# RWKV attention and a mixture of experts on one core: the attention periods' steps in a new order, with a chunk's preceding sums added by two transfers in place of one

## The reference, cut to what matters

```python
xk = x * time_mix_k + shifted * (1 - time_mix_k)      # xv, xr alike
k, v, r = xk @ Wk.T, xv @ Wv.T, xr @ Wr.T
# per token, with num, den, mx carried along:
mo  = maximum(mx, kt + u)
out = (exp(mx - mo) * num + exp(kt + u - mo) * vt) / (exp(mx - mo) * den + exp(kt + u - mo))
ms  = maximum(mx + w, kt)
num = exp(mx + w - ms) * num + exp(kt - ms) * vt       # den alike, without vt
y = (sigmoid(r) * out) @ Wo.T
```

## Time and profile before

| what | us |
|---|---|
| median of 3 runs | 1244.07 (1239.03 to 1246.96) |
| the profiled execution | 1250.05 |
| its span, first to last instruction | 1248.3 |
| from the start to the last `refined` of the attention | 511.3 |

### The profile page before, as it was taken

One profiled execution on the slowest core, in us unless ns is written; L12 is line 12 of the kernel. 1 busy time (PEld: TensorE's weight loads), 2 busy tenths in 40 slices (PEclk: granted clock), 3 DMA queues, 4 the chain that ended last, 5 costly groups with the idle time before them and its releaser, 6 DMA issues.

```text
span 1248.3 us, 16083 instructions
## 1 busy us (share of the span) xinstructions
PE 1117.1 (89%) x5320; PEld 832.2 (67%) x5320; DVE 838.5 (67%) x1951; ACT 750.2 (60%) x1279; POOL 331.8 (27%) x295
## 2 busy tenths in 40 slices
PE   5969989899989967899999889999998998999893
PEld 3546646473646544488888778888887886878761
DVE  4798988888798877689887944454444444444384
ACT  2666979698888888653332245565565555546353
POOL 2021121212222121200000034433434443344355
PEclk9989999899999977899999999999999999999996
DMA  8412364453635266676363069979888987887798
GB/s 320 175 34 67 56 158 71 138 101 102 140 76 105 68 142 157 151 218 241 139 208 111 5 213 244 256 239 257 247 231 263 245 240 235 220 243 185 186 317 329
DMA packets 87972, 222.52 MB, mean 178 GB/s; under 512 B 10704, under 2 KB 10832, under 8 KB 85072
## 3 DMA queue, kind: packets, MB, share of 16 engines
q1 hardware_dynamic: 59424, 156.98, 35.8%
q0 software_dynamic: 28464, 64.50, 28.0%
HBM read 145.93 MB, written 59.28 MB: 164 GB/s over the span
## 4 chain that ended last, share of the span: by engine, by line
PE 28%; DMA 18%; DVE 6%; issue 3%; ACT 2%; POOL 1%; POOLq 0%; SPq 0%; DVEq 0%; ACTq 0%
DMA ysh<-k_sb,mixf 13%; PE bank L734 5%; PE bank L709 3%; PE bank L711 2%; PE bank L710 2%; PE bank L691 2%; PE bank L692 2%; PE bank L693 2%; DMA xnd<-ysh 2%; DMA xnd<-h,mixf 1%; PE bank L537 1%; PE bank L723 1%; PE bank L749 1%; PE bank L751 1%; PE bank L750 1%
## 5 line engine op out<-in xcount | busy, mean ns | idle before, releaser
L1387 POOL DMA_INDIRECT ysh<-k_sb,mixf x64 | 115.7, 1807 | 202.3 <-DMA ysh<-k_sb,mixf 115.3
L598 PE MATMUL bank<-mix_ring,weights 128*128 128x512 f32 x288 | 133.5, 617 | 19.4 <-DVE mix_ring L1489 19.4
L605 PE MATMUL bank<-weights,rw 128*128 128x512 f32 x256 | 118.8, 620 | 13.8 <-ACT sr L863 11.4
L1133 ACT ACTIVATE k_sb<-bank 128x512 f32<-128x512 f32 x64 | 38.2, 597 | 140.5 <-PE bank L693 140.5
L598 PEld LDWEIGHTS bank<-mix_ring,weights 128*128 128x128 f32 x288 | 56.3, 198 | 91.1 <-issue 67.4
L1363 POOL DMA_INDIRECT xres<-h,mixf x48 | 54.1, 1127 | 221.7 <-DVE mixf L1928 210.4
L1942 DVE TENSOR_TENSOR run_max<-run_max 128x256 f32<-128x256 f32 x64 | 27.3, 426 | 118.9 <-ACT e_split L1169 118.9
L1327 POOL DMA_DIRECT2D wkv<-recur x31 | 38.0, 1225 | 254.5 <-DVE recur L1554 254.5
L691 PE MATMUL bank<-h_high,ffn_w 128*128 128x512 f32 x256 | 102.7, 401 | 2.7 <-ACT k_sb L1133 2.7
L605 PEld LDWEIGHTS bank<-weights,rw 128*128 128x128 f32 x256 | 50.9, 200 | 78.5 <-issue 63.5
L709 PE MATMUL bank<-ffn_w,s_split 128*128 128x512 f32 x256 | 101.9, 398 | 0.1
(11 more groups left out here) (253 smaller groups left out, 2737.4 us busy)
## 6 DMA issues: line engine op xcount, KB each, us to landing
wkv<-in_w SPq DMA_DIRECT2D x96, 512.0 KB, 5.1
state<-in_w SPq DMA_DIRECT2D x32, 512.0 KB, 4.7
wkv<-recur POOLq DMA_DIRECT2D x31, 512.0 KB, 5.3
h<-xres SPq DMA_DIRECT2D x8, 1024.0 KB, 4.2
xin<-h SPq DMA_DIRECT2D x8, 1024.0 KB, 6.3
xin<-in_x SPq DMA_DIRECT2D x7, 1024.0 KB, 9.3
xres<-in_x POOLq DMA_DIRECT2D x7, 1024.0 KB, 11.7
x<-xres SPq DMA_DIRECT2D x7, 1024.0 KB, 4.5
```

Source lines behind the costliest of these rows:

```text
L598: mm = pe.matmul(bank[:, d, :], W(j)[:, ck, d * P:(d + 1) * P], mix_slot(4 * j + ck), start=(ck == 0), stop=(ck == CK - 1))
L605: mm = pe.matmul(bank[:, s, :], rw[:, ck, s * P:(s + 1) * P], W(3)[:, ck, :], start=(ck == 0), stop=(ck == CK - 1))
L1387: pool.indirect_dma_start(t["ysh"], bass.IndirectOffsetOnAxis(ap=scatter_token[:, e % IB:e % IB + 1], axis=0), e_out[q], None, compute_op= ...
```

## The change

In all four blocks the helper functions are cut into single steps (one instruction or one chunk each; each returns at once where its tile does not exist), and `period` is a plain list of them in a new order. PE's list is in the old order; its waits for a PSUM half are replaced by a wait for each bank ahead of the first matmul into it. `add_prev` issues two accumulating transfers of 256 KB. `den_scan` loses its wait for `boosted`, and `y_squares` its wait for `x1_squared` (the latter has a scratch tile of its own, `x1_junk`). The first and the last periods get their extra steps at other places. Some semaphores are merged to make room for two new ones. No arithmetic changes.

PE, the waits for one bank at a time (k, transposed x and y alike):

```diff
-            def output(bank, tau, ck):
+            def output(tau, ck):
                 pe.wait_ge(S["rw_ready"], 4 * tau + ck + 1)
                 for s in range(ST):
+                    if ck == 0:
+                        if has(tau, 1):
+                            pe.wait_ge(S["r_ready"], 4 * (tau + 1) + s + 1)
...
```

POOL:

```diff
             def add_prev(tau, c):
                 u = CK * tau + c
+                pool.wait_ge(S["boosted"], u + 1)
                 pool.wait_ge(S["r_times_v"], u + 1)
+                pool.wait_ge(S["scanned"], 2 * u + 1)
+                pool.dma_start(unit[:, c % 2, R, :], sums_of[:, c % 2, 1, 0:TT], accum_op=ALU.add).then_inc(S[f"den_added{u % 2}"], 16)
                 pool.wait_ge(S["scanned"], 2 * u + 2)
-                pool.dma_start(unit[:, c % 2, NUM:R + 1, :], sums_of[:, c % 2, :, 0:TT], accum_op=ALU.add).then_inc(S[f"prev_added{u % 2}"], 16)
+                pool.dma_start(unit[:, c % 2, NUM, :], sums_of[:, c % 2, 0, 0:TT], accum_op=ALU.add).then_inc(S[f"num_added{u % 2}"], 16)
...
+                if has(tau, 0): add_prev(tau, 0)
+                if has(tau, 2) and not first(tau): scale_and_offset(1, tau + 2)
...
```

ACT, the new list of a middle period (steps of the first and the last periods left out):

```diff
+                v_round(tau + 1, 0)
+                if has(tau, 0): ln3_row(tau - 2, 0)
+                if has(tau, 0): ln3_row(tau - 2, 1)
...
+                if has(tau, 0): ln3_row(tau - 2, 2)
+                above(tau, 1)
+                below(tau, 1)
+                carry_over(tau, 0)
+                exp_both(tau, 1)
+                room(tau, 1)
+                if has(tau, 0): ln3_row(tau - 2, 3)
+                boost(tau, 1)
+                v_round(tau + 1, 1)
+                v_round(tau + 1, 2)
...
+                seed(tau, 2)
+                recip_log(tau, 0)
...
+                ln1_row(tau + 2, 0)
+                ln1_row(tau + 2, 1)
+                ln1_row(tau + 2, 2)
+                k_read(even, tau + 1, 0)
+                k_read(even, tau + 1, 1)
+                ln1_row(tau + 2, 3)
+                k_read(even, tau + 1, 2)
+                k_read(even, tau + 1, 3)
...
+                recip_exp(tau, 0)
+                above(tau, 2)
+                below(tau, 2)
+                carry_over(tau, 1)
+                exp_both(tau, 2)
+                if has(tau, 0): y_square(tau - 1, 0)
...
+                v_round(tau + 1, 3)
+                if has(tau, 0): y_square(tau - 1, 3)
+                room(tau, 2)
+                recip_log(tau, 1)
+                seed(tau, 3)
+                boost(tau, 2)
+                r_round(tau + 1, 0)
...
+                recip_exp(tau, 1)
+                if has(tau, 0): y_scale(tau - 1, 0)
...
+                r_round(tau + 1, 1)
+                v_read(tau + 1, 0)
...
+                above(tau, 3)
+                r_round(tau + 1, 2)
+                below(tau, 3)
+                r_round(tau + 1, 3)
+                xnT_read(tau + 2, 0)
...
+                exp_both(tau, 3)
+                carry_over(tau, 2)
+                room(tau, 3)
+                boost(tau, 3)
+                seed(tau + 1, 0)
...
+                recip_log(tau, 2)
+                recip_exp(tau, 2)
...
+                if has(tau, 0): x1_square(tau - 1, 0)
+                if has(tau, 0): x1_square(tau - 1, 1)
+                if has(tau, 0): x1_square(tau - 1, 2)
...
+                above(tau + 1, 0)
+                below(tau + 1, 0)
+                exp_both(tau + 1, 0)
+                r_reads(tau + 1)
+                if has(tau, 0): x1_square(tau - 1, 3)
+                room(tau + 1, 0)
+                boost(tau + 1, 0)
+                carry_over(tau, 3)
+                recip_log(tau, 3)
+                recip_exp(tau, 3)
...
+                seed(tau + 1, 1)
```

DVE, the same (`e_times_v` is line 1533 of before, `recip_times_sum` and `recip_times_num` are 1578 and 1580):

```diff
+                if not first(tau): ln1_row_stats(tau + 2, 0)
+                mix(tau + 1, VJ, 0)
+                if not first(tau): ln1_row_stats(tau + 2, 1)
+                den_scan(tau, 0)
+                e_times_v(tau, 0)
+                r_times_v(tau, 0)
+                num_scan(tau, 0)
...
+                gap_scan(tau, 1)
...
+                gap_taken(tau, 1)
...
+                if not first(tau): recip_times_num(tau - 1, 3)
...
+                if not first(tau): ln1_moments(tau + 2)
+                if not first(tau): recip_times_sum(tau - 1, 3)
...
+                if not first(tau): refined(tau - 1, 3)
+                mix(tau + 1, VJ, 1)
+                mix(tau + 1, VJ, 2)
+                den_scan(tau, 1)
...
+                v_rest(tau + 1, 2)
...
+                num_gated(tau, 0)
...
+                recip_times_sum(tau, 0)
+                recip_times_num(tau, 0)
+                mix(tau + 1, VJ, 3)
+                refined(tau, 0)
+                mix(tau + 1, RJ, 0)
+                den_scan(tau, 2)
...
+                v_rest(tau + 1, 3)
+                mix(tau + 1, RJ, 1)
+                e_times_v(tau, 2)
+                num_scan(tau, 2)
+                r_rest(tau + 1, 0)
+                r_times_v(tau, 2)
+                mix(tau + 1, RJ, 2)
+                gap_scan(tau, 3)
+                mix(tau + 1, RJ, 3)
+                gap_taken(tau, 3)
+                shift(tau + 2)
+                r_rest(tau + 1, 1)
+                num_gated(tau, 1)
+                recip_times_sum(tau, 1)
+                recip_times_num(tau, 1)
+                r_rest(tau + 1, 2)
+                refined(tau, 1)
+                diff(tau + 2, 0)
+                diff(tau + 2, 1)
+                r_rest(tau + 1, 3)
+                mix(tau + 2, KJ, 0)
+                den_scan(tau, 3)
+                e_times_v(tau, 3)
+                r_times_v(tau, 3)
+                num_scan(tau, 3)
+                gap_scan(tau + 1, 0)
+                gap_taken(tau + 1, 0)
...
+                mix(tau + 2, KJ, 1)
+                num_gated(tau, 2)
...
+                num_gated(tau, 3)
...
+                mix(tau + 2, KJ, 3)
```

703 lines of the change are left out of this document (352 added, 351 removed).

## The result

The kernel after takes 1195.6 us (median of 4 runs, 1192.1 to 1200.0) where the kernel before, run beside it, takes 1245.5: ratio 0.9595, 95% interval 0.9523 to 0.9666.

A forecast was written before the change was run, and what follows sets the result against it. PE was taken to bound the kernel, with 52.8 us the least per middle period. Gains of 18.4 + 0.5 + 4.0 + 7.6 = 30.5 took 1250.05 to 1219.5, minus 6.0 to 1213.5, stated as 1215 us; range 1203 to 1237.

The forecast's parts named there:

- The chain through the residual and the seed: Middle periods: with the seed ahead of `x1_square`, PE's `mix_ring` wait goes; periods fall from 58.6 to 54.0, 18.4 us.
- PE's least: Middle periods: PE is busy 52.8 us at full clock, so no period can be shorter than 52.8.
- Fifth period: The period with no tile left to normalise, 53.3 us long, gains 0.5 us.
- Period 0: Statistics of tile 2 move ahead of four mixes; PE's v starts at 77.2, not 82.80; 4.0 us counted, between 1 and 7.
- The finer waits of PE: PE waits per PSUM bank: up to 1.6 us where ACT is late, in middle periods inside the 54.0.
- The split: Two transfers per unit for one: early denominator worth nothing, price nothing up to a landing of about 7 us.
- The last two periods: Attention's end: 1 for PE's reads of r, 4.2 for `boosted`, 2.4 for two moved steps; 7.6 us, bounds 0 and 12.
- The wait for `boosted`: Last tile: `den_scan` waits for `exped` instead, 1.4 us earlier for three units, 4.2 us.
- (a): Rival, middle periods: the loops of PE, DVE and ACT disturb each other; periods of 56.5, time 1230 us; chance 0.20.
- (b): Rival: residual lands later, ACT stands at `x1_square`, PE's wait moves and keeps its length; 1238 us; chance 0.12.
- (c): Rival: a fixed time per transfer makes the second half 2.8 us later, `seed(tau, 2)` 1.5 late; 1222 us; chance 0.10.
- (d): Rival, slower: two halves land at 16 us or later, ACT stands at `seed(tau+1, 0)`; 1260 us; chance 0.08.

The follow-up runs named there:

- e2: Kernel after with ACT's seed of the next tile's unit 0 put back behind three of the four x1 squares; 1208.7 us, ratio 0.9707.
- e3: Kernel before with ACT's seed of the next tile's unit 0 put ahead of the four x1 squares; 1229.6 us, ratio 0.9872.
- e17: Kernel after with the residual's 1 MB transfer issued as two of 512 KB, the first two x1 squares waiting for the first alone; 1195.4 us, ratio 0.9597.
- e5: Kernel after, but PE waits for all four banks of a PSUM half ahead of the first matmul into it; 1199.1 us, ratio 0.9634.
- e8: Kernel after with one transfer of 512 KB per unit in tiles 0 to 5 and two of 256 KB in tiles 6 and 7; 1199.1 us, ratio 0.9629.
- e14: Kernel after with one accumulating transfer of 512 KB per unit in place of two, same code as e1; 1203.5 us, ratio 0.9665.
- e6: Kernel after with `den_scan` waiting for `boosted` again; 1238.6 us, ratio 0.9939.
- e9: Kernel before, order kept, but the denominator scan no longer waits for `boosted`; e*v waits for `room`, r*v for `boosted`; 1245.7 us, ratio 1.0019.
- e15: Kernel after with each of a unit's two transfers cut in two, four of 128 KB; 1205.9 us, ratio 0.9690.
- e1: Kernel after with one accumulating transfer of 512 KB per unit in place of two; 1201.8 us, ratio 0.9665.

## Why the prediction came out too small, point by point

**The chain through the residual and the seed: right.** The wait for `mix_ring` went, the granted clock is 1.00 in every middle period, and the seed is there before `gap_scan`, as the walk had it. e2 and e3 show it from both sides. It isn't the whole of the middle's gain: alone it earns 2.7 of the 6.0 us a period (e3).

**PE's least: the step that failed.** The forecast said that "a middle period can't be shorter than 52.8" and set 54.0 on it. e17's periods of 50.3 refute it. The row of 57.60 us in the earlier trace rows has two marks that I passed over. It counts 180 PE records, where the others have 176 to 178 and a period's own are 176 (32 each of k and of output, 48 each of v and of r, 16 transposes): the cut caught four matmuls of v more. And PE stood three times in it, and each restart adds to "busy" time: the groups of k took 3.59 and 7.13 us around a wait, where the same 24 records in one run take 10.46 (PE's timelines of before and after). Four records at 0.23 us and, as an estimate, three restarts at those 0.26 make 1.7 of the 2.5; the rest I did not trace. With PE's 52.8 out of the way, DVE's loop was the bound; the walk had 52.1 for it and it is 52.4. With 52.1 as the base the same sum gives 52.1 + 1.2 = 53.3, so that of the 1.4 us a period 0.7 go to PE's least and 0.7 to the 1.2 for "delays of one pass to another". Together they are 4 x (54.0 - 52.6), 5.5 us of the miss.

**Fifth period: "PE's full work does fit into 53" was the same error.** Its 50.75 of PE in 53.3 left room for 2.5, and I gave it 0.5. It gained 4.1 and is now 49.2 long, below those 50.75. 3.6 us of the miss.

**Period 0: right mechanism, mis-sized.** v starts at 76.20 (said 77.2), 6.6 us earlier. The 2.4 us held back for `ffn_rest` were wrong: at the period's end nothing waits for it, and PE runs from 81.2 to 132.8 without a stop. The gain was 7.2, at the upper bound of 7. 3.2 us of the miss.

**The finer waits of PE: right for the middle, short for the ends.** In the middle nothing (e5). At the ends about 1.5 and 5 us in one profile of e5, of which the forecast had counted a part in period 0; the times don't show them.

**The split: half right.** "The early denominator is worth nothing in this order" holds for middle periods of 52.3 us, and there "the price of the split is also nothing" holds too (e8, e14). The +0.8 us for the second half was too careful: a half lands in 4.0, so the second lands about as early as the whole did. In the tail the split is worth 5.2 us, most of it through the numerator of unit (6, 3) and about 2 through the denominator of unit (7, 1). What failed in this part is a term of the last two periods, where I named the landing of unit (6, 3)'s sums and counted "nothing beyond 1". Rival (e), the split doing nothing, falls.

**The last two periods.** 10.0 in place of 7.6, and the terms can't be checked one by one against it. Put back into the new order, the whole transfer costs 5.2 us of this stretch (e14), the wait for `boosted` over 7 (e6) and the coarse waits of PE 5.0 (e5), over 17 together: they overlap. In the old order taking `boosted` away gave 1.3 (82.5 in e9), against the 4.2 of the forecast. That the sum came within 2.4 us of the measured gain is therefore luck in part. PE's wait for r fell from 11.42 to 5.73, the routing's from 9.33 to 8.61.

**The wait for `boosted`.** The forecast used it in the last tile only. Shown is that nearly the whole gain of the new order hangs on its going (e6, 38 to 43 us), and that in the old order it is worth nothing (e9). Pricing a change edit by edit, each against the old order, can't find this.

**The rivals.** (a), loops in each other's way, did not happen: 52.6. (b) was the right place with a small price: the residual does land later (13.3), ACT does stand there, and the period pays 2 us for it (e17), not the whole gain. (c) and (d): no wait of a seed for its sums shows in the kernel after or in e15 with its four transfers. The Trainium skill (DMA: Bandwidth & Descriptors, section on the anatomy of one DMA on the SWDGE path) would make a half 0.6 us shorter than a whole, an estimate from its 436 GB/s; the rows have 5.3, 4.0 and 3.5 us for 512, 256 and 128 KB, 1.3 and 0.5 us less. The same page of the Trainium skill, in its rules for kernel authors, advises to coalesce many small transfers into one large one; here two of 256 KB in place of one of 512 KB earn 5 us of the tail in the profile.

**The scale.** The 6.0 us by which the profile of before lay over the median match the part behind the attention, which was at the long end there (737.0 of 724 to 737), so subtracting them fits the record. The misses are 5.5 + 3.6 + 3.2 + 2.4 = 14.7; with the 1.5 added for small waits they make 16.2 of the 19.4 us from 1215 to 1195.6. The other 3 are within the scatter of the medians (1195.6 and 1200.7 for the same kernel). The low end of the range counted a gain of 41 us; the attention gained 45.0, and what lies beyond is the fifth period's 3.6.

## What to carry to other kernels

PE's busy time in a window is no floor while PE still stops in it: compare the record counts and add up an unbroken run of each kind of matmul. Price a removed wait in the new order, not in the old: the same wait was worth 0 us in one and about 40 in the other. Where engines are within 5% of each other, look for the last wait on a transfer in the loop and try letting its first users wait for the first half only (e17: 2.1 us a period in the profile, not shown in the time). Here a split transfer shortened the stretch where a unit's chain stands alone, and in e15 it cost through its issues on the queue, by what stood behind them.

## What the runs showed of the hardware beyond that

The residual's transfer of 1 MB landed in 10.9 to 13.3 us (medians) over the kernels above, and in 11.9 and 12.9 in two executions of one kernel (e1, e14), whose middle periods were 51.5 and 52.3. Over the kernels with ACT's middle list unchanged and one residual transfer the middle period lies between 51.0 and 52.6. As two of 512 KB it lands in 9.5 us each by the median. From 81 to 343 us POOL is busy 1.23 us for an issue of 512 KB alone (e14), 0.91 and 0.95 for two of 256 KB, and 1.06 and 1.71 each in the first and second pair of 128 KB (e15). The residual's issue behind them took 1.64, 2.00 and 2.69 us: in these rows an issue takes longer the more stand directly ahead of it. What made the landing scatter stays open.
